# Moving the normalisation's two elementwise passes from VectorE to GpSimd in a post-LayerNorm transformer layer

## The chip, the cores and the metric

The kernel runs on all 8 cores of one Trainium2 chip, each core on its own 2048 of the 16384 token rows, with no traffic between the cores. The time is device microseconds of the slowest core. The hardware profiler also took one execution, whose trace of the slowest core (core 3) is what is read here. An instruction is named by its line in the kernel: L1282 is the instruction issued at line 1282. Engines: PE is TensorE, DVE is VectorE, ACT is ScalarE, POOL is GpSimd, and SP is SyncE, which only issues transfers here.

## What is computed

One layer: attention, residual, LayerNorm, a gated feed-forward with ternary weights, residual, LayerNorm.

```python
def _layernorm(x, axis=-1, eps=1e-5):
    m = jnp.mean(x, axis=axis, keepdims=True)
    v = jnp.var(x, axis=axis, keepdims=True)
    return (x - m) / jnp.sqrt(v + eps)

...
x = _layernorm(x + _L0_attn_ref(x, Wq, Wk, Wv, Wo), axis=-1)
x = _layernorm(x + _L0_ffn_ref(x, w1, w2, w3), axis=-1)
```

Here x is 2 x 8192 x 2048 in float32. `_L0_attn_ref` projects to q, k and v, rotates a part of q and k, and applies softmax attention and the output projection. `_L0_ffn_ref` rounds its weights to -1, 0 and 1 and computes (sigmoid(x w1) * x w2) w3. There are 16 heads, and the feed-forward is 5632 wide.

## The kernel before

Activations lie transposed: 128 partitions hold 128 of the 2048 features, and tokens run along the free axis. So a LayerNorm sums over partitions. It does so with matmuls against a vector of ones, which leave the sum and the sum of squares as one row of 512 tokens; five small DVE instructions and two ACT instructions turn these into -mean and 1/std, two matmuls spread each over 128 partitions into PSUM, and two ACT copies bring them to SBUF as `nm_sb` and `rs_sb`. Then every feature block j (16 of them) is normalised with two passes, `y = y + nm_sb` and `out = y * rs_sb`, each on 128 x 512 elements in float32. These two passes, for one block a "pair" below, are what the change is about.

Everything is written as one instruction stream for each engine, in program order, with semaphores between the engines. No scheduler reorders anything: an instruction that waits holds up all that stands behind it on its engine, transfers too. On DVE, ACT and POOL every instruction also waits for the one before it on the same engine, by a chain semaphore (Vch, Sch, Gch).

- **P0 and P1** (projections, weight statistics, attention) are not touched.
- **P3** (`emit_p3`) is the output projection and the first LayerNorm. It goes over 4 chunks t of 512 tokens. In each it runs 16 units, one for each block j: POOL issues the load of the weights `wot` (L916), SP that of the residual `xto` (L921), PE runs 16 matmuls (L933), DVE adds the residual (L945) and casts (L953), ACT squares (L955), and PE adds to the two sums (L964, L967). The weights have two buffers, so the load for unit u waits until unit u-2 has left PE; the PSUM tiles also have two buffers, so PE runs at most two units ahead of L945. After 16 units come the statistics (L974 to L1005) and the 16 pairs (L1015, L1017). SP stores each result to `x1scr` (L1019), from two staging buffers. In POOL's stream and in SP's, the loads of chunk t+1 stand behind all that chunk t issued there.
- **P4** (`emit_p4`) is the feed-forward and the second LayerNorm, in two halves of 1024 tokens. Each half loads `x1scr` (SP, L1074), and runs 44 steps in which POOL loads `w1t` and `w2t` (L1085, L1089), ACT and DVE quantise them (L1100 to L1113), and PE multiplies (L1128, L1133). Then it multiplies with `w3` (L1177), adds the residual (L1191) and writes the sum to `y2scr` in HBM. At the end of a half come, for each of two token chunks tc, the statistics (L1237 to L1268) and 16 pairs (L1282, L1285). Here the data come back from HBM: SP issues load j (L1278), the pair runs, SP issues store j (L1288), and only behind it in SP's stream stands load j+1.

```python
                    aw = [("p4fs", f4), ("p4ev", self.val("p4ev"))] + spill_done
                    if len(fin_rec) >= 2:
                        aw.append(fin_rec[-2])
...
                            waits=aw, inc=f"p4y2r{par}", inc_amt=16)
```

So the first load of a chunk waits for the statistics too (`f4` is the second ACT copy, L1268).

Of the kernel before, what the change touches and what calls it, by code (L numbers as in the profile page):

```python
# [55 lines left out]
class KB:  # L56
# [829 lines left out]
    def emit_p3(self):  # L886
# [22 lines left out]
        for t in range(4):  # L909
            for j in range(16):  # L910
# [8 lines left out]
                        waits=ww, inc=f"p3dma{par}", inc_amt=16)  # L919
# [3 lines left out]
                        waits=xw, inc=f"p3xd{par}", inc_amt=16)  # L923
# [17 lines left out]
                ybuf = self.f32v(o_y[j], 512)  # L941
                sttw = [("p3mm", mm), xd_]
                if t >= 1:
# [3 lines left out]
                        waits=sttw, inc="p3ev")  # L947
# [23 lines left out]
            while p3pend:  # L971
                p3pend.pop(0)()
            sw = [("p3smm", self.val("p3smm"))]
            self.op("vector", lambda E: E.tensor_scalar(  # L974
# [27 lines left out]
            st3 = self.val("p3st")  # L1002
            self.op("scalar", lambda E: E.copy(out=self.nm_sb, in_=self.pv(1024, 512)),
                    waits=[("p3st", st3)])
            self.op("scalar", lambda E: E.copy(out=self.rs_sb, in_=self.pv(1536, 512)),  # L1005
                    inc="p3st")
            st4 = self.val("p3st")
            for j in range(16):
# [4 lines left out]
                if len(x1st_rec) >= 2:  # L1013
                    aw.append(x1st_rec[-2])
                self.op("vector", lambda E, y=ybuf: E.tensor_tensor(  # L1015
                    out=y, in0=y, in1=self.nm_sb, op=ALU.add), waits=aw)
                self.op("vector", lambda E, y=ybuf, o=x1s: E.tensor_tensor(  # L1017
                    out=o, in0=y, in1=self.rs_sb, op=ALU.mult), inc="p3a")
# [12 lines left out]
    def emit_p4(self):  # L1031
# [38 lines left out]
        for half in range(2):  # L1070
# [163 lines left out]
            for tc in range(2):  # L1234
                sbase = 3072 if tc == 0 else 2048
                sw = [("p4smm", self.val("p4smm"))]
                self.op("vector", lambda E, sb=sbase: E.tensor_scalar(  # L1237
# [28 lines left out]
                self.op("scalar", lambda E: E.copy(out=self.nm_sb, in_=self.pv(1024, 512)),  # L1266
                        waits=[("p4fs", f3)])
                self.op("scalar", lambda E: E.copy(out=self.rs_sb, in_=self.pv(1536, 512)),  # L1268
                        inc="p4fs")
                f4 = self.val("p4fs")  # L1270
                for j in range(16):
# [4 lines left out]
                    if len(fin_rec) >= 2:  # L1276
# [4 lines left out]
                            waits=aw, inc=f"p4y2r{par}", inc_amt=16)  # L1281
                    self.op("vector", lambda E, y=y2: E.tensor_tensor(  # L1282
                        out=y, in0=y, in1=self.nm_sb, op=ALU.add),
                            waits=[(f"p4y2r{par}", self.val(f"p4y2r{par}"))])
                    self.op("vector", lambda E, y=y2, o=outst: E.tensor_tensor(  # L1285
                        out=o, in0=y, in1=self.rs_sb, op=ALU.mult), inc="p4a")
# [71 lines left out]
```

How the kernel before makes its waits and increments, by code:

```python
        def fn(E, SH, _w=tuple(phys_waits), _mk=make, _u=upd):  # L90
            for s, v in _w:
                E.wait_ge(SH[s], v)
            ins = _mk(E)
            if _u is not None:
                ins.then_inc(SH[_u[0]], _u[1])
# [52 lines left out]
        def fn(E, SH, _w=tuple(fw)):  # L148
            for s, v in _w:
                E.wait_ge(SH[s], v)
```

## Time and profile before

| | us |
|---|---|
| median of 2 runs | 12654.13 (12580.48 and 12727.78) |
| the profiled execution | 12302.35 |
| its span, core 3 | 12300.4 |
| spans of the 8 cores | 12165.6 to 12300.4 |
| P0 and P1 | about 7946 |
| P3 | about 592 |
| P4, two halves | about 3762 |

The table's stages are read from the trace of core 3. The span is the time from its first instruction to its last, 2 us less than the time of the same execution. The two timed runs lie 2.3% and 3.5% above the profiled one.

### The profile page before, as it was taken

How to read it: one execution, taken by the hardware profiler on the slowest of the kernel's cores; microseconds unless marked ns; L12 is line 12 of the kernel's file. 1: busy time of each engine (PE TensorE's matmuls, PEld its weight loads, DVE VectorE, ACT ScalarE, POOL GpSimd, SP SyncE). 2: the span in 40 equal slices, each digit the busy share in tenths (PEclk: the TensorE clock that was granted, in tenths of full speed). 3: DMA queues.
4: the chain of work that ended last, by engine and by line, in shares of the span. 5: the costliest groups of instructions: out<-in, count | busy, mean ns of one | idle time of the engine just before them, and what ended most of it. 6: DMA issues, size and time to landing. Idle time of an engine off the chain costs nothing.

```text
span 12300.4 us, 106356 instructions; the slowest of 8 cores (12165.6 to 12300.4 us)
## 1 busy us (share of the span) xinstructions
PE 8438.9 (69%) x34596; PEld 3306.7 (27%) x34596; DVE 4556.7 (37%) x4760; ACT 3940.6 (32%) x3777; POOL 456.6 (4%) x409
## 2 busy tenths in 40 slices
PE   6768668777766088888888888855555681555582
PEld 2223223323322033333333333221222230222231
DVE  2403304214013177777777777633111101111101
ACT  2012012011132266666666666501333200333200
POOL 0000000000000000000000000011000000000000
PEclk9889889888878599999999999977777895777886
DMA  7446355364364400100100100176222223222222
GB/s 140 101 92 142 86 105 120 77 121 104 73 126 97 130 17 27 40 14 27 40 14 27 40 14 27 22 101 106 75 75 75 76 79 87 73 75 75 81 77 61
DMA packets 833313, 904.52 MB, mean 74 GB/s; under 512 B 412672, under 2 KB 713728, under 8 KB 808960
## 3 DMA queue, kind: packets, MB, share of 16 engines
q0 software_dynamic: 471232, 356.54, 17.3%
q1 hardware_dynamic: 361536, 541.18, 14.2%
q8 instruction: 285, 4.67, 0.2%
q14 instruction: 260, 2.13, 0.1%
HBM read 908.07 MB, written 161.48 MB: 87 GB/s over the span
## 4 chain that ended last, share of the span: by engine, by line
PE 50%; ACT 15%; DMA 15%; DVE 10%; issue 4%; another core or an unknown queue 3%; SPq 2%; ACTq 0%; DVEq 0%; POOL 0%; POOLq 0%
PE pp L597 7%; PE pp L430 7%; ACT arena L815 7%; PE pp L800 6%; PE pp L1128 6%; PE pp L805 5%; PE pp L1133 5%; PE pp L1177 5%; DMA arena<-w3t 3%; PE pp L838 2%; DMA arena<-wvt 2%; PE pp L834 2%; DMA arena<-y2scr 2%; DVE arena L317 2%
## 5 line engine op out<-in xcount | busy, mean ns | idle before, releaser
L825 DVE TENSOR_TENSOR arena<-arena 128x1024 f32<-128x1024 f32 x2016 | 2469.4, 1225 | 529.4 <-ACT arena L815 430.5
L815 ACT ACTIVATE arena<-pp,arena 128x1024 bf16<-128x1024 f32 x2048 | 2282.6, 1115 | 886.8 <-PE pp L838 585.9
L430 PE MATMUL pp<-arena 128*128 128x512 bf16 x7680 | 1808.6, 392 | 347.0 <-DMA arena<-wkt 279.9
L800 PE MATMUL pp<-arena 128*128 128x512 bf16 x4096 | 1586.5, 387 | 270.5 <-ACT arena L815 113.2
L1128 PE MATMUL pp<-arena 128*128 128x512 bf16 x2816 | 807.7, 451 | 1230.4 <-DVE arena L1113 1055.1
L805 PE MATMUL pp<-arena 128*128 128x512 bf16 x4096 | 1589.8, 388 | 0.0
L597 PE MATMUL pp<-arena 128*128 128x512 bf16 x4096 | 922.0, 389 | 290.9 <-DMA arena<-wvt 290.9
L430 PEld LDWEIGHTS pp<-arena 128*128 128x128 bf16 x7680 | 739.3, 100 | 1340.5 <-issue 574.6
L317 DVE TENSOR_REDUCE arena<-arena 128x1 f32<-128x2816 f32 (+1 forms) x108 | 298.1, 2760 | 1548.5 <-DMA arena<-w3t 549.4
L834 PE MATMUL pp<-arena 128*128 128x512 bf16 x2048 | 780.6, 381 | 29.8 <-ACT arena L815 29.5
L838 PE MATMUL pp<-arena 128*128 128x512 bf16 x2048 | 778.1, 380 | 0.0
L1128 PEld LDWEIGHTS pp<-arena 128*128 128x128 bf16 x2816 | 309.5, 112 | 1716.4 <-issue 1505.1
L800 PEld LDWEIGHTS pp<-arena 128*128 128x128 bf16 x4096 | 399.5, 98 | 1361.1 <-issue 1126.7
L1177 PE MATMUL pp<-arena 128*128 128x512 bf16 x2816 | 681.0, 405 | 93.3 <-DMA arena<-w3qg 93.1
L1143 DVE TENSOR_TENSOR arena<-pp,arena 128x512 bf16<-128x512 f32 x176 | 121.7, 691 | 1465.0 <-ACT arena L1140 1465.0
L604 ACT CAST arena<-pp 128x512 bf16<-128x512 f32 x256 | 150.0, 586 | 1600.7 <-PE pp L597 1600.7
L1133 PE MATMUL pp<-arena 128*128 128x512 bf16 x2816 | 636.5, 379 | 0.0
L597 PEld LDWEIGHTS pp<-arena 128*128 128x128 bf16 x4096 | 407.5, 100 | 804.8 <-issue 346.0
L1140 ACT ACTIVATE arena<-pp 128x512 f32<-128x512 f32 x176 | 105.1, 597 | 1478.3 <-PE pp L1133 1478.3
L462 DVE TENSOR_REDUCE arena<-pp 1x1 f32<-1x512 f32 x400 | 271.5, 679 | 735.9 <-PE pp L454 610.9
L805 PEld LDWEIGHTS pp<-arena 128*128 128x128 bf16 x4096 | 400.3, 98 | 272.0 <-issue 36.3
L484 ACT CAST arena<-pp 128x512 bf16<-128x512 f32 x256 | 150.0, 586 | 966.2 <-PE pp L430 966.2
(124 smaller groups left out, 5106.7 us busy)
## 6 DMA issues: line engine op xcount, KB each, us to landing
arena<-w3t SPq DMA_DIRECT2D x88, 1024.0 KB, 5.8
arena<-w1t POOLq DMA_DIRECT2D x88, 1024.0 KB, 8.0
arena<-w2t POOLq DMA_DIRECT2D x88, 1024.0 KB, 10.0
arena<-wkt POOLq DMA_DIRECT2D x96, 512.0 KB, 10.0
kscr<-arena SPq DMA_DIRECT2D x384, 128.0 KB, 2.0
arena<-w1t SPq DMA_DIRECT2D x32, 1408.0 KB, 6.6
arena<-w2t SPq DMA_DIRECT2D x32, 1408.0 KB, 6.7
arena<-w3qg SPq DMA_DIRECT2D x32, 1408.0 KB, 13.0
```

The costliest lines, as they stand in the source:

```text
L317: self.op("vector", lambda E, n=ncols: E.tensor_reduce(out=self.gred_tmp, in_=gt[:, 0:n], axis=AX.X, op=ALU.add, apply_absolute_value=True ...
L430: self.op("tensor", lambda E, f=f, ps=ps, t=wk, lo=tok_lo, n=ntok: E.matmul(ps, t[:, f * 128:(f + 1) * 128], xh[:, f * 2048 + lo: f * 2048 ...
L597: self.op("tensor", lambda E, f=f, ps=psV, tb=tb, t=wv: E.matmul(ps, xh[:, f * 2048 + tb * 128: f * 2048 + tb * 128 + 128], t[:, f * 512:( ...
L800: kn=kn, qn=qn: E.matmul(ps[:, hf * 512:(hf + 1) * 512], kn[:, kb * 128:(kb + 1) * 128], qn[:, q0:q0 + 512], start=True, stop=False), waits=w)
L805: kr=kr, qr=qr: E.matmul(ps[:, hf * 512:(hf + 1) * 512], kr[:, kb * 128:(kb + 1) * 128], qr[:, q0:q0 + 512], start=False, stop=True),
L815: self.op("scalar", lambda E, ps=psS, pt=ptile: E.activation(out=pt, in_=ps, func=AF.Exp, bias=self.negmh_bc, scale=1.0), waits=ew, inc="p ...
L825: self.op("vector", lambda E, pt=ptile: E.tensor_tensor(out=lacc, in0=lacc, in1=pt, op=ALU.add), waits=lw, inc="p1l")
L834: self.op("tensor", lambda E, pt=pt, kb=kb, vh=vh2, vo=vo: E.matmul(self.pv(2048, 512), vh[:, kb * 256 + vo:kb * 256 + vo + 128], pt[:, 0: ...
L838: self.op("tensor", lambda E, pt=pt, kb=kb, vh=vh2, vo=vo: E.matmul(self.pv(2560, 512), vh[:, kb * 256 + vo:kb * 256 + vo + 128], pt[:, 51 ...
L1128: self.op("tensor", lambda E, f=f, ps=psA, tc=tc, w1q=w1q: E.matmul(ps, w1q[:, f * 128:(f + 1) * 128], x1h[:, f * 1024 + tc * 512: f * 102 ...
L1133: self.op("tensor", lambda E, f=f, ps=psB, tc=tc, w2q=w2q: E.matmul(ps, w2q[:, f * 128:(f + 1) * 128], x1h[:, f * 1024 + tc * 512: f * 102 ...
L1177: self.op("tensor", lambda E, f=f, ps=psF, tc=tc, jj=jj: E.matmul(ps, w3sl[:, f * 512 + jj * 128: f * 512 + jj * 128 + 128], hsb[:, f * 10 ...
```

## The change

The two passes of both LayerNorms are issued on `gpsimd` in place of `vector`: 64 pairs in P3 and 64 in P4, 256 instructions. Everything that DVE's own order used to guarantee is now a wait: the first statistics instruction (L974, L1237) waits for the earlier statistics to be used up, and the ACT copy that overwrites `nm_sb` (L1003, L1266) waits until the last pairs that read it are done.

```diff
-            sw = [("p3smm", self.val("p3smm"))]
+            sw = [("p3smm", self.val("p3smm")), ("p3st", self.val("p3st"))]
...
             self.op("scalar", lambda E: E.copy(out=self.nm_sb, in_=self.pv(1024, 512)),
-                    waits=[("p3st", st3)])
+                    waits=[("p3st", st3), ("p3a", self.val("p3a")), ("p4a", self.val("p4a"))])
...
-                self.op("vector", lambda E, y=ybuf: E.tensor_tensor(
+                self.op("gpsimd", lambda E, y=ybuf: E.tensor_tensor(
                     out=y, in0=y, in1=self.nm_sb, op=ALU.add), waits=aw)
-                self.op("vector", lambda E, y=ybuf, o=x1s: E.tensor_tensor(
+                self.op("gpsimd", lambda E, y=ybuf, o=x1s: E.tensor_tensor(
                     out=o, in0=y, in1=self.rs_sb, op=ALU.mult), inc="p3a")
...
-                sw = [("p4smm", self.val("p4smm"))]
+                sw = [("p4smm", self.val("p4smm")), ("p4fs", self.val("p4fs"))]
...
                 self.op("scalar", lambda E: E.copy(out=self.nm_sb, in_=self.pv(1024, 512)),
-                        waits=[("p4fs", f3)])
+                        waits=[("p4fs", f3), ("p4a", self.val("p4a"))])
...
-                    self.op("vector", lambda E, y=y2: E.tensor_tensor(
+                    self.op("gpsimd", lambda E, y=y2: E.tensor_tensor(
                         out=y, in0=y, in1=self.nm_sb, op=ALU.add),
                             waits=[(f"p4y2r{par}", self.val(f"p4y2r{par}"))])
-                    self.op("vector", lambda E, y=y2, o=outst: E.tensor_tensor(
+                    self.op("gpsimd", lambda E, y=y2, o=outst: E.tensor_tensor(
                         out=o, in0=y, in1=self.rs_sb, op=ALU.mult), inc="p4a")
```

The first place is POOL's stream in P3. Before, it holds the 64 weight loads in one run, and the first loads of P4 right behind them:

```order
L754 MEMSET arena 128x8192 [waits Gch]
L916 DMA arena<-wot 128x16x128 [waits Vch]
L916 DMA arena<-wot 128x16x128
L916 DMA arena<-wot 128x16x128 [waits p3mm] x62
L1085 DMA arena<-w1t 128x16x128 [waits p3mm]
L1089 DMA arena<-w2t 128x16x128
```

Now the 16 pairs of chunk 0 stand between its loads and those of chunk 1, and so at every chunk's end:

```order
L916 DMA arena<-wot 128x16x128 [waits Vch]
L916 DMA arena<-wot 128x16x128
L916 DMA arena<-wot 128x16x128 [waits p3mm] x14
L1015 TENSOR_TENSOR arena<-arena 128x512 [waits Vch,Sch,p3st,Gch]
L1017 TENSOR_TENSOR arena<-arena 128x512 [waits Gch]
...
L1015 TENSOR_TENSOR arena<-arena 128x512 [waits p3x11,Gch]
L1017 TENSOR_TENSOR arena<-arena 128x512 [waits Gch]
L916 DMA arena<-wot 128x16x128 [waits p3mm] x16
```

The two loads that used to be issued while the pairs ran are moved behind them. In the same way the loads of `w1t` and `w2t` for a half of P4 now stand behind the pairs of P3's last chunk, and behind the 32 pairs of the first half.

The second place is DVE's stream at the end of a half of P4. Before, the pairs of chunk tc=0 stand between the statistics of the two chunks:

```order
L1237 TENSOR_SCALAR arena<-pp 1x512 [waits p4smm,Vch]
...
L1247 TENSOR_SCALAR arena<-arena 1x512 [waits Vch]
L1282 TENSOR_TENSOR arena<-arena 128x512 [waits p4y2r0,Vch]
L1285 TENSOR_TENSOR arena<-arena 128x512 [waits Vch]
...
L1237 TENSOR_SCALAR arena<-pp 1x512 [waits Vch]
```

Now the second chunk's statistics follow the first's, with a wait for ACT and PE (p4fs) in front:

```order
L1237 TENSOR_SCALAR arena<-pp 1x512 [waits p4smm,Vch]
...
L1247 TENSOR_SCALAR arena<-arena 1x512 [waits Vch]
L1237 TENSOR_SCALAR arena<-pp 1x512 [waits Vch,Sch,p4fs]
...
L1247 TENSOR_SCALAR arena<-arena 1x512 [waits Vch]
L1104 TENSOR_TENSOR arena<-arena 128x2048 [waits Sch,p4mm,Vch]
```

So the statistics of tc=1 no longer stand behind 32 passes. PE's stream is the same as before.

## Rows read from the trace of the kernel before

**Rows 1.** The page: the chain that ended last, by engine.
```profile
PE 50%; ACT 15%; DMA 15%; DVE 10%; issue 4%; another core or an unknown queue 3%; SPq 2%; ACTq 0%; DVEq 0%; POOL 0%; POOLq 0%
```
**Rows 2.** Windows: us, busy and count of PE, PEld, DVE, ACT, POOL; PEclk, DMA share, GB/s.
```profile
8062.00:8110.00 48.00, 13.47 (x41) 4.78 (x40) 26.78 (x39) 3.15 (x5) 3.43 (x3) 0.66 0.46 74
10171.00:10423.00 252.00, 8.79 (x13) 2.57 (x12) 54.52 (x78) 14.96 (x14) 3.44 (x3) 0.51 0.38 97
```
**Rows 3.** Groups by line: busy us, mean ns, then idle before and its releasers.
```profile
L1282 DVE TENSOR_TENSOR arena<-arena 128x512 f32<-128x512 f32 x64 | 44.3, 692 | 344.7 <-DMA arena<-y2scr 344.7
L1015 DVE TENSOR_TENSOR arena<-arena 128x512 f32<-128x512 f32 x64 | 44.3, 692 | 62.1 <-DMA x1scr<-arena 30.5 <-ACT arena L1005 29.0 <-DVE arena L1017 2.4
L1285 DVE TENSOR_TENSOR arena<-arena 128x512 f32<-128x512 f32 x64 | 44.3, 692 | 7.0 <-DVE arena L1282 0.5
```
**Rows 4.** Groups by line and form, POOL alone.
```profile
L754 POOL MEMSET arena<- 128x8192 bf16 x1 | 6.9, 6928 | 0.1
L754 POOL MEMSET arena<- 128x2048 bf16 x2 | 3.6, 1809 | 345.8 <-DMA w3qg<-arena 345.7
```
**Rows 5.** Timeline, P4's first pair: start us, length us, instruction, [idle before].
```profile
10189.40 0.69 DVE L1282 TENSOR_TENSOR arena<-arena 128x512 f32<-128x512 f32 x1 [11.66 <-DMA arena<-y2scr]
10190.96 0.34 SPq L1288 DMA_DIRECT2D out<-arena  x1
10191.35 0.42 SPq L1278 DMA_DIRECT2D arena<-y2scr  x1
```
**Rows 6.** Timeline, between the pairs of tc=0 and tc=1, first half.
```profile
10289.19 0.68 DVE L1237 TENSOR_SCALAR arena<-pp 1x512 f32<-1x512 f32 x1
...
10298.42 0.59 ACT L1266 COPY arena<-pp 128x512 f32<-128x512 f32 x1 [4.09 <-PE pp L1262]
...
10299.86 0.32 SPq L1278 DMA_DIRECT2D arena<-y2scr  x1
```
**Rows 7.** Timeline, P3: SP's run of 16 stores in each chunk.
```profile
8077.30 32.62 SPq L1019 DMA_DIRECT2D x1scr<-arena  x16
...
8218.28 32.55 SPq L1019 DMA_DIRECT2D x1scr<-arena  x16
...
8367.11 32.40 SPq L1019 DMA_DIRECT2D x1scr<-arena  x16
...
8511.77 26.38 SPq L1019 DMA_DIRECT2D x1scr<-arena  x16
```
**Rows 8.** The chain in order of time, P3: start us, length us, what.
```profile
8037.64 7.99 DMA arena<-wot
...
8128.35 5.30 PE pp L933 x16
...
8141.49 5.32 PE pp L933 x16
...
8272.71 6.49 PE pp L933 x16
...
8417.98 5.32 PE pp L933 x16
```
**Rows 9.** Timeline, the start of P4's two halves.
```profile
8559.55 6.41 PE L1128 MATMUL pp<-arena 128*128 128x512 bf16 x16 [50.94 <-DMA arena<-x1scr]
...
10405.50 0.43 SPq L1074 DMA_DIRECT2D arena<-x1scr  x1
...
10422.69 4.99 PE L1128 MATMUL pp<-arena 128*128 128x512 bf16 x16 [124.36 <-DMA arena<-x1scr]
```
**Rows 10.** The page: issues, KB each, median us from issue to landing.
```profile
arena<-w1t POOLq DMA_DIRECT2D x88, 1024.0 KB, 8.0
arena<-w2t POOLq DMA_DIRECT2D x88, 1024.0 KB, 10.0
```
**Rows 11.** Groups by line: a sign pass and a quantising add of P4.
```profile
L1108 ACT ACTIVATE arena<-arena 128x2048 bf16<-128x2048 f32 x88 | 176.1, 2001 | 267.5 <-DVE arena L1104 267.5
L1104 DVE TENSOR_TENSOR arena<-arena 128x2048 bf16<-128x2048 bf16 x88 | 107.8, 1225 | 307.7 <-ACT arena L1102 307.5
```

## The prediction

> **What bounds the kernel now.** I read the page first. The chain that ended last is half PE, then ACT and DMA, with DVE at 10% and POOL at 0% [rows 1]. An average over stages says little about 256 instructions, so I went to the stretches where they run, by windows. In a chunk's end in P3 (48 us) PE is busy 13.5 us and POOL 3.4; between the halves of P4 (252 us) PE is busy 8.8 us and POOL 3.4 [rows 2]. There nothing else works: the pairs are on the path, and no matmul hides them. It is also where POOL looks free, so the question is what the pairs cost there, and what they push back.
>
> What ends the waits differs between the two places [rows 3]. In P4 each of 64 pairs waits for its own load from `y2scr` (344.7 us in all, 5.4 each), and the timeline shows a closed ring: L1282 starts at 10189.40, the store is issued 1.56 us later, and the next load only behind it at 10191.35 [rows 5]. Load, two passes, store issue, next load: a pass that gets longer makes the ring longer by just that. In P3 the data are in SBUF and the pairs wait little (30.5 us for staging buffers, 29.0 for the statistics): the passes themselves are most of it.
>
> **The cost of a pass on POOL.** On DVE one takes 0.692 us [rows 3]. No row shows a two-input pass on POOL, so I bound it. POOL's memsets take 1.809 us for 2048 bf16 elements and 6.928 for 8192 [rows 4]: 0.833 ns for each further element and 0.10 us fixed. One stream of 512 elements would be 0.53 us; that is the lower end, 0.16 under DVE. Three streams (two read, one written) that take turns, each float32 element counted as two bf16 ones, would be 0.10 + 3 x 512 x 2 x 0.833 ns = 2.66 us; that is the upper end. If an element costs the same in either type, reads in turn with the write beside them give 0.10 + 0.85 = 0.95 us, and all three in turn 1.38 us. The memsets are the only rows of this engine, and I see no reason for counting bytes rather than elements, so I take the middle of these two, 1.15 us. Call x what a pair gains in length: 2 x (1.15 - 0.69) = 0.92 us, between -0.33 and +3.94. The chain semaphore costs a gap on POOL as it does on DVE; I take it as equal.
>
> Twice the DVE row would be 1.38 us, which is my three streams in turn. The Trainium skill speaks against the change: its GPSIMD Engine Reference, in Performance versus the Vector engine, says that a two-input elementwise operation is about half as fast on GPSIMD, since its two reads share one port, and gives 4497 ns against 2293 ns for 2048 float32 elements. A quarter of 4497 ns is an estimate of 1.12 us, by which the sum below would be 7 us less; its ratio of 1.96 on our row is an estimate of 1.36 us, by which it would be the first rival. No row here shows which.
>
> **The terms.**
>
> 1. *P4's pairs.* 64 rings, each longer by x: 64 x 0.92 = 59 us. All are on the path: the 32 of the first half too, since `x1scr` for the second half is loaded by SP behind them (10405.50), and PE waits 124 us for it [rows 9].
>
> 2. *P3's pairs.* SP's 16 stores of a chunk are issued over 32.6, 32.6, 32.4 and 26.4 us [rows 7], 15 steps each. The last chunk's pace, 1.76 us, is that of the passes with little waiting. The three before it run at 2.17, since transfers of `wot` then share the DMA engines with the stores. On POOL no `wot` is under way then (next term), so all four would run at 1.76 + x = 2.68, which also gives each store longer to land: 40.2 us. That is +7.7 for three and +13.8 for the last, and x more in each for the first pair: 3 x 8.6 + 14.7 = 41 us. In general this term is 64x - 18.
>
> 3. *Loads behind the pairs in P3.* Before, the loads for units 0 and 1 of the next chunk are issued as the last units end, those for 2 and 3 while the pairs run, so units 2 and 3 start at once when the residual has come. Unit 4, the first that waits for its weights, starts 18.4, 21.9 and 18.5 us after the last store is issued (8128.35 - 8109.92, 8272.71 - 8250.83, 8417.98 - 8399.51) [rows 7, 8]. After the change the load for unit 0 is issued only when the pairs are done. It lands 8.0 us later, and from there two units take 13.1 us, bound by such loads (8141.49 - 8128.35) [rows 8]: unit 4 starts at 7.8 + 26.3 = 34.1 us. The loss is 15.7 + 12.2 + 15.6 = 43 us. What DVE gains does not help: L945 is free to run, but there is no product for it. The bounds are 30 us, if loads land in 6 us when nothing else moves, and 48.
>
> 4. *Statistics of tc=1 in P4.* From L1237 at 10289.19, right after the last pair of tc=0, to the load at 10299.86 are 10.7 us, of which the two ACT copies and the issue at the end are 1.4 (from 10298.42) [rows 6]. With DVE free, all up to the copies is done while POOL works through tc=0's pairs. Only the copies, which wait for these pairs, stay: -9.2 us for each half, -18.4 us. The gain is bounded by these 9.2, and nothing queued behind the waiting copy on ACT is needed earlier: the sign passes of the next half have no weights yet. In P3 no such gain exists, since a chunk's statistics need its own matmuls.
>
> 5. *Loads of `w1t` and `w2t` behind the pairs.* Before, they had long landed, and PE waited for `x1scr`: 21.4 us after the last store of P3 was issued, and 17.2 us after the issue of the load in the second half [rows 7, 9]. Now they are issued when the last pair ends and land 8.0 and 10.0 us after issue [rows 10]; then four sign passes and two adds follow, 4 x 2.0 + 2 x 1.2 = 10.5 us with little between [rows 11]: about 20 to 21 us, if `x1scr`, 4 MB, does not slow them. It will: 6 MB share the engines where 4 MB took 17.2 us, which at the same rate is 26 us. I take +8 for the first half and +11 for the second, 19 us; the bounds are 0 and 30, the upper end with the weights landing only behind `x1scr`.
>
> The new waits in front of L974 and L1237 are met when they are reached in P3 (the last broadcast is a whole chunk old), and in P4 lie inside term 4. Other edits have no price.
>
> Sum: 59 + 41 + 43 - 18 + 19 = 144; as a formula it is 128x + 26. Against the profiled execution's own 12302 us that is 12446. The median of the runs shown is 12654, 352 us higher, for which the trace has no row; I put the same 144 us on top of it: 12798 us, or 1.1%.
>
> **Rivals.**
>
> - *A pass takes 1.38 us*, twice the DVE row. Then x = 1.38 and the sum is 128 x 1.38 + 26 = 203 us: 12857, 1.6%. For it: two reads and a write in turn. The skill's ratio of about two, in the same place of the GPSIMD Engine Reference, would put it here. Chance 0.20.
> - *POOL is much slower*, over 1.6 us a pass: this is the case on the other side. With x above 1.78 the sum passes 253 us, which is 2%. Two float32 reads in turn counted by bytes are 0.10 + 1.71 = 1.81 us, x = 2.24, +313 us: 12967. For it: the memset's rate is known for a 2-byte type alone. Against it: it needs POOL at 2.6 times DVE's time. Chance 0.14.
> - *The freed DVE pays.* If the next chunk's units could run beside the pairs, the idle 33 us of PE in each of three boundaries would go: terms 2 and 3 become about 15 - 99 = -84, and the sum 59 - 84 - 18 + 19 = -24 us: 12630. For it: PE is idle there [rows 2]. Against it: both streams that feed these units, POOL's and SP's, hold their loads behind the pairs. Chance 0.04.
> - *POOL is as fast as DVE* or faster: x near 0 gives +26, x = -0.33 gives -16: 12638 to 12680. Chance 0.07.
>
> **How the numbers follow.** The forecast keeps 0.55, with x from 0.5 to 1.2 and so +90 to +180. The range reaches down through the two cheap cases to 12600, which is -54, about their lower end with terms 3 and 5 at theirs, and up to the 1.81 us pass, 12965; about 0.12 lies outside. A measurement of this kernel can tell some 2% (253 us) from no change. Faster by more than that: 0.01, since even the lowest bound is under 1%. Slower: 0.14 for the slow pass and 0.01 for terms 3 and 5 at their worst beside a dear pass, 0.15. Within 2%: 0.84.
>
> **What would show each step.** In the trace after: the mean of L1015 and L1282 on POOL (1.15; the price of a pass); the run of 16 stores, 40 us in every chunk (term 2); POOL's first `wot` issue behind the last L1017, and unit 4 34 us after the last store (term 3); L1237 of tc=1 starting while the pairs of tc=0 run, and 1.4 us between the last pair and the load (term 4); PE's first L1128 waiting for L1113 or for `x1scr`, 25 to 30 us after the last pair (term 5). The forecast is wrong if the pass is off by half a microsecond, or if a ring in P4 grows by something other than the two passes, such as a slower hand-over from POOL to SP.

## The result, and the profile after

| | before | changed |
|---|---|---|
| median of all its runs, us | 12677.99 (10 runs, 12275.55 to 12846.53) | 12550.24 (11 runs, 12444.93 to 12963.89) |
| comparable runs, changed / before | | **1.0153**, 95% interval 1.0105 to 1.0201 |
| span of the profiled execution's slowest core | 12300.4 | 12444.2 |
| span of its median core | 12194.7 | 12421.6 |

Some executions of either kernel run at a lower clock and take some per cent longer, so only undisturbed ones are compared, and the two medians of all runs say nothing. On 12302 us the ratio is +188 us (+129 to +247): slower, and by less than the 2% that was called a difference, which the upper end of the interval (2.01%) just reaches. The two profiled spans differ by 144 us, the very sum of the prediction, but that is chance: core 3 of the kernel before ended 106 us behind its median core, core 4 of the changed one 23 us behind. Between median cores it is +227 us. I work below with medians over the eight cores of the times between named instructions:

| stretch, us | before | changed | difference |
|---|---|---|---|
| P3 (first L933 to P4's first L1128) | 603.0 | 724.8 | +121.8 |
| closing block of the first half (first `y2scr` load to the issue of the last store) | 185.3 | 228.4 | +43.1 |
| last store's issue to the second half's first L1128 | 18.9 | 29.4 | +10.5 |
| closing block of the second half (to the end) | 185.7 | 233.5 | +47.8 |

These four make 223 of the 227 us. The page of the changed kernel (span; busy times; the chain by engine):

```profile
span 12444.2 us, 105745 instructions; the slowest of 8 cores (12388.3 to 12444.2 us)
PE 8328.7 (67%) x33908; PEld 3296.5 (26%) x34596; DVE 4378.3 (35%) x4504; ACT 3938.0 (32%) x3777; POOL 779.3 (6%) x665
PE 50%; ACT 15%; DMA 14%; DVE 8%; issue 5%; another core or an unknown queue 3%; POOL 3%; SPq 2%; ACTq 0%; DVEq 0%; POOLq 0%
```

Against [rows 1], POOL has come onto the chain with 3% and DVE has left it with 2: the pairs stayed on the path when they changed engine. One window between the halves (us; busy time and count of PE, PEld, DVE, ACT, POOL; granted clock, DMA share, GB/s), core 4:

```profile
10290.00:10545.00 255.00, 3.75 (x4) 1.16 (x4) 0.00 (x0) 1.35 (x3) 80.42 (x64) 0.50 0.35 82
```

It answers to the second of [rows 2]: DVE does nothing at all now, PE next to nothing (3.75 us), and POOL is busy for under a third of the time. The groups by line (busy us, mean ns of one, idle before and its releasers), core 4:

```profile
L1282 POOL TENSOR_TENSOR arena<-arena 128x512 f32<-128x512 f32 x64 | 80.8, 1262 | 1196.5 <-DMA arena<-y2scr 1196.5
L1285 POOL TENSOR_TENSOR arena<-arena 128x512 f32<-128x512 f32 x64 | 80.7, 1260 | 9.2
L1017 POOL TENSOR_TENSOR arena<-arena 128x512 bf16<-128x512 f32 x64 | 80.6, 1260 | 9.2
L1015 POOL TENSOR_TENSOR arena<-arena 128x512 f32<-128x512 f32 x64 | 80.6, 1260 | 115.5 <-ACT arena L1005 106.9
L1266 ACT COPY arena<-pp 128x512 f32<-128x512 f32 x4 | 2.3, 585 | 228.5 <-POOL arena L1285 220.1 <-PE pp L1262 8.4
```

A pass takes 1260 ns, whether it writes float32 or bf16; on DVE it took 692 [rows 3]. The idle time of 1196.5 us in front of L1282 is no cost to read: POOL waits there through each half as well, where before DVE had other work. The timeline of core 4 (start us, length us, instruction, [idle before]) shows the places of [rows 5 to 9]:

```profile
8050.22 42.42 SPq L1019 DMA_DIRECT2D x1scr<-arena  x16
8092.19 2.36 POOL L916 DMA_DIRECT2D arena<-wot  x2
8101.84 9.93 PE L933 MATMUL pp<-arena 128*128 128x512 bf16 x32 [55.97 <-DMA arena<-wot]
...
8131.00 5.30 PE L933 MATMUL pp<-arena 128*128 128x512 bf16 x16 [3.82 <-DMA arena<-wot]
...
8590.00 42.42 SPq L1019 DMA_DIRECT2D x1scr<-arena  x16
8631.97 1.21 POOL L1085 DMA_DIRECT2D arena<-w1t  x1
8634.13 0.37 SPq L1074 DMA_DIRECT2D arena<-x1scr  x1
8644.95 2.00 ACT L1100 ACTIVATE arena<-arena 128x2048 bf16<-128x2048 f32 x1 [58.02 <-DMA arena<-w2t]
8656.33 5.71 PE L1128 MATMUL pp<-arena 128*128 128x512 bf16 x16 [70.80 <-DVE arena L1113]
...
10294.08 1.26 POOL L1282 TENSOR_TENSOR arena<-arena 128x512 f32<-128x512 f32 x1 [4.37 <-DMA arena<-y2scr]
10295.48 1.26 POOL L1285 TENSOR_TENSOR arena<-arena 128x512 f32<-128x512 f32 x1
10296.81 0.34 SPq L1288 DMA_DIRECT2D out<-arena  x1
10297.24 0.39 SPq L1278 DMA_DIRECT2D arena<-y2scr  x1
...
10398.81 1.26 POOL L1285 TENSOR_TENSOR arena<-arena 128x512 f32<-128x512 f32 x1
10400.16 0.58 ACT L1266 COPY arena<-pp 128x512 f32<-128x512 f32 x1 [109.98 <-POOL arena L1285]
10401.60 0.32 SPq L1278 DMA_DIRECT2D arena<-y2scr  x1
...
10558.21 5.39 PE L1128 MATMUL pp<-arena 128*128 128x512 bf16 x16 [264.04 <-DVE arena L1113]
```

The reader is to see four things. The ring is the same, with 3.16 us from the first pass to the next load where it had 1.95 [rows 5]. PE waits 56 us at a P3 boundary for `wot`, whose loads POOL issues only at 8092.19, behind the last pass; unit 4 starts 38.4 us after the last store (8131.00 - 8092.64). Between tc=0 and tc=1 only the copies are left, 1.5 us from the store's issue to the load. And both halves of P4 now wait for quantised weights (L1113), not for `x1scr` as in [rows 9].

### The profile page after: what moved, and what is told of

Read it like the earlier page. It is cut to its first block, busy times and chain, and to the rows that moved or that the text cites. A ratio compares the mean times of both kernels' runs of the same rounds, so it can differ in the third digit from the quotient of the medians.

```text
span 12444.2 us, 105745 instructions; the slowest of 8 cores (12388.3 to 12444.2 us)
## 1 busy us (share of the span) xinstructions
PE 8328.7 (67%) x33908; PEld 3296.5 (26%) x34596; DVE 4378.3 (35%) x4504; ACT 3938.0 (32%) x3777; POOL 779.3 (6%) x665
## 4 chain that ended last, share of the span: by engine, by line
PE 50%; ACT 15%; DMA 14%; DVE 8%; issue 5%; another core or an unknown queue 3%; POOL 3%; SPq 2%; ACTq 0%; DVEq 0%; POOLq 0%
PE pp L430 7%; PE pp L597 7%; ACT arena L815 7%; PE pp L1128 6%; PE pp L800 6%; PE pp L805 5%; PE pp L1133 5%; PE pp L1177 5%; DMA arena<-w3t 3%; PE pp L838 2%; DMA arena<-y2scr 2%; DMA arena<-wot 2%; DMA arena<-wvt 2%; PE pp L834 2%
## 5 line engine op out<-in xcount | busy, mean ns | idle before, releaser
L1128 PE MATMUL pp<-arena 128*128 128x512 bf16 x2762 | 799.9, 452 | 1404.0 <-DVE arena L1113 1398.9
L805 PE MATMUL pp<-arena 128*128 128x512 bf16 x4096 | 1589.1, 388 | 50.9 <-DMA arena<-kscr 25.8
L1128 PEld LDWEIGHTS pp<-arena 128*128 128x128 bf16 x2816 | 310.8, 113 | 1881.1 <-issue 1667.8
L834 PE MATMUL pp<-arena 128*128 128x512 bf16 x1970 | 750.3, 381 | 29.7 <-ACT arena L815 29.4
L604 ACT CAST arena<-pp 128x512 bf16<-128x512 f32 x256 | 149.8, 585 | 1590.1 <-PE pp L597 1590.1
L1143 DVE TENSOR_TENSOR arena<-pp,arena 128x512 bf16<-128x512 f32 x176 | 121.8, 692 | 1439.6 <-ACT arena L1140 1439.6
L933 PE MATMUL pp<-arena 128*128 128x512 bf16 x1001 | 289.4, 452 | 312.5 <-DMA arena<-wot 310.2
```

Of the source, the lines that this page charges most:

```text
L805: kr=kr, qr=qr: E.matmul(ps[:, hf * 512:(hf + 1) * 512], kr[:, kb * 128:(kb + 1) * 128], qr[:, q0:q0 + 512], start=False, stop=True),
L834: self.op("tensor", lambda E, pt=pt, kb=kb, vh=vh2, vo=vo: E.matmul(self.pv(2048, 512), vh[:, kb * 256 + vo:kb * 256 + vo + 128], pt[:, 0: ...
L1128: self.op("tensor", lambda E, f=f, ps=psA, tc=tc, w1q=w1q: E.matmul(ps, w1q[:, f * 128:(f + 1) * 128], x1h[:, f * 1024 + tc * 512: f * 102 ...
```

## The experiments

Each leaves the computation as it is. "Land" is the time from a `y2scr` load's issue to the first pass, "pass part" from there to the next load's issue; both are medians over cores of each core's mean. A diff is against the changed kernel where nothing else is said.

### One place at a time

In `x1_p4_only` P3's pairs are back on DVE, in `x2_p3_only` P4's are. The lines are those of P3; in P4 the same two words change:

```diff
-                self.op("gpsimd", lambda E, y=ybuf: E.tensor_tensor(
+                self.op("vector", lambda E, y=ybuf: E.tensor_tensor(
...
-                self.op("gpsimd", lambda E, y=ybuf, o=x1s: E.tensor_tensor(
+                self.op("vector", lambda E, y=ybuf, o=x1s: E.tensor_tensor(
```

> Only the pairs of P4 on POOL, those of P3 back on DVE. Stage figures are medians over the 8 cores, from before and after: the closing block of a half of P4 (first y2scr load to last store issued) took 185 us before and 228 (first half) after, a ring 5.46 and 7.14 us. Theory (a ring pays the length of its two passes, 2 x (1.26 - 0.69) and two gaps, 1.24 us, and nothing else): each block is longer by 32 x 1.24 - 9.2 = 30 us, the start of the second half by 10; P3 stays at 603 us; in all +70 us. Rival (on POOL the ring also pays a slower hand-over or slower loads, as the 1.68 us between the two traces suggest): blocks +43 to +48, in all +100 us.

> Only the pairs of P3 on POOL. Theory (the terms of the two LayerNorms are independent): P3, from its first L933 to the first L1128, takes 725 us as after the change against 603 before, so +120 us; the closing blocks of P4 stay at 185 us, with 10.7 us between the pairs of the two chunks. Rival (P3's loss comes from the whole change, by transfers or clock): P3 well under 725. The two kernels, P4 alone and P3 alone, should add up to the change: about +190 to +230.

On their chip the kernel before took 12245 us (median of four comparable runs). `x1_p4_only`: 12307, +62. Its blocks took 215.6 and 218.8 us (+30 and +33), the second half started after 29.4 us, as in the changed kernel, and P3's runs of stores were those of before (the whole of P3, 636 us at a granted clock of 0.74 over that trace, is not comparable with the 603). `x2_p3_only`: 12309 and 12393, +64 and +148; its P3 took 707.0 us (+104, where I had expected +120), its runs of stores 42.1 us in all four chunks, and the second half started after 18.8. Its closing blocks did not stay at 185 us: they took 203.9 and 199.0, with the pairs on DVE, because its `y2scr` loads landed late (3.84 us where the kernel before has 3.45, in the table below). The two halves add up to +126 to +210 us, beside the change's +188. So each half of the change brings its own loss, and the late weights of the second half belong to P4's pairs. The groups of `x1_p4_only` (core 6) show the two engines in one kernel:

```profile
L1282 POOL TENSOR_TENSOR arena<-arena 128x512 f32<-128x512 f32 x64 | 81.2, 1269 | 1220.6 <-DMA arena<-y2scr 1220.6
L1015 DVE TENSOR_TENSOR arena<-arena 128x512 f32<-128x512 f32 x64 | 44.3, 692 | 63.2 <-DMA x1scr<-arena 31.2 <-ACT arena L1005 29.0 <-DVE arena L1017 2.9
```

### The loads, and the statistics

`x3_loads_first` issues the next loads ahead of the pairs (P4's first `w1t` and `w2t` likewise):

```diff
+            if t < 3:
+                wot_load(16 * t + 16)
+                wot_load(16 * t + 17)
+            else:
+                self.p4_first_load()
             for j in range(16):
```

> The changed kernel, but POOL issues the next stage's first loads (wot for units 0 and 1 of the next chunk, w1t and w2t of the next half) ahead of the pairs. Theory (the loads queued behind the pairs cost 53 us in P3 and 10 + 2 us at the starts of the halves): unit 4's end after the last store of a chunk goes from 44 back to 26 us, P3 from 725 to about 672, the start of the second half from 29.4 to 19 us, in all -65 us against the changed kernel, and what is left, about +125 against before, is the price of the passes. Rival (POOL's descriptor work for the loads is itself slowed beside the passes, or the stores suffer): P3 stays above 690.

P3 fell from 724.8 to 685.7 us, and the start of the second half from 29.4 to 21.0; P4's first start is that of before again (21.9). The one comparable run took 12400. Its timeline on core 1:

```profile
8032.10 1.14 POOL L912 DMA_DIRECT2D arena<-wot  x1 [8.21 <-PE pp L940]
8036.18 1.15 POOL L912 DMA_DIRECT2D arena<-wot  x1 [2.94 <-PE pp L940]
...
8047.69 8.63 PE L940 MATMUL pp<-arena 128*128 128x512 bf16 x32
8049.38 1.26 POOL L1027 TENSOR_TENSOR arena<-arena 128x512 f32<-128x512 f32 x1 [12.04 <-ACT arena L1012]
...
8094.10 2.35 POOL L912 DMA_DIRECT2D arena<-wot  x2
```

The products of units 0 and 1 (8047.69) now run before the pairs begin. Units 2 and 3 still get their weights at 8094.10, behind the pairs, since all loads stand in POOL's order. The order of issue on POOL, not POOL's work as such, cost 39 us of P3 and 8 of P4; 83 us of P3's loss stay with the loads in front. I had expected 53 us back in P3. At the three boundaries unit 4's residual add (L945) ends 29 us after the last store, against 43 to 44 in the changed kernel and 25 to 26 before, which is 43 of the 53 us; what is left fits the late weights of units 2 and 3. Elsewhere P3 was some 6 us slower than in the changed kernel, 2 of them in the last run of stores (43.9 us).

`x4_stats_first` is the kernel before, on DVE, with tc=0's pairs emitted behind the statistics of tc=1:

```diff
+                if tc == 1:
+                    pairs0()
                 self.op("scalar", lambda E: E.copy(out=self.nm_sb, in_=self.pv(1024, 512)),
```

> All pairs on DVE as before, but in P4 the statistics of the second token chunk stand ahead of the pairs of the first, on DVE, ACT and PE; only the copies into nm_sb and rs_sb wait for those pairs. Theory (the 9.2 us that the change wins in each half is a matter of order, not of the engine): the gap goes from 10.7 to 1.5 us in each half, in all -18 us. Rival: the five statistics instructions ahead of the first pair delay it and give 3.5 us of each 9.2 back, -11 us; or the gain needs a free DVE, 0.

The gap between the pairs fell from 10.7 to 1.6 us, and the blocks from 185.3 and 185.7 to 175.0 and 173.7. It had no comparable run, so it is read by blocks alone. The one gain of the change is a matter of order: DVE gives it too, without POOL.

### What a pass costs in the ring

`x5_third_pass` issues the second pass of P4's pairs twice, on POOL:

```diff
+                    self.op("gpsimd", lambda E, y=y2, o=outst: E.tensor_tensor(
+                        out=o, in0=y, in1=self.rs_sb, op=ALU.mult))
                     self.op("gpsimd", lambda E, y=y2, o=outst: E.tensor_tensor(
                         out=o, in0=y, in1=self.rs_sb, op=ALU.mult), inc="p4a")
```

> The changed kernel with the second pass of every P4 pair done twice on POOL (the same product again, so the output is the same). The runs so far give a ring of 6.4 to 6.6 us on cores whose loads are not disturbed with the passes on POOL, and 5.3 with them on DVE. Theory (the ring pays the passes one for one): one pass and its gap more, 1.40 us, ring 7.8 to 8.0, each closing block +45 us (32 x 1.40), +90 in all. Rival (part of the pass hides beside the load, or the excess of the first comparison is a cost of each POOL instruction): ring +0.7 or less, or +1.7 and more.

```profile
10340.00 1.26 POOL L1282 TENSOR_TENSOR arena<-arena 128x512 f32<-128x512 f32 x1 [3.85 <-DMA arena<-y2scr]
10341.41 1.26 POOL L1285 TENSOR_TENSOR arena<-arena 128x512 f32<-128x512 f32 x1
10342.81 1.26 POOL L1287 TENSOR_TENSOR arena<-arena 128x512 f32<-128x512 f32 x1
10344.14 0.34 SPq L1290 DMA_DIRECT2D out<-arena  x1
10344.57 0.38 SPq L1278 DMA_DIRECT2D arena<-y2scr  x1
```

This is its timeline on core 5: 4.57 us from the first pass to the next load, 1.41 more than with two. The blocks took 258 us, which is only 30 and 25 more than in the changed kernel's first trace, where I had expected 45: the loads landed 0.47 us earlier in this one, and 32 x (1.41 - 0.47) is 30. Taken apart, the ring reads:

| us | pass part | land |
|---|---|---|
| before; `x4_stats_first`; `x2_p3_only` (DVE) | 2.00; 2.01; 2.01 | 3.45; 3.39; 3.84 |
| changed; `x1_p4_only`; `x3_loads_first`; `x12_changed_again` (POOL) | 3.18; 3.18; 3.19; 3.18 | 3.93; 3.54; 3.34; 3.56 |
| `x5_third_pass` (POOL, three passes) | 4.59 | 3.46 |

The pass part is the same on all eight cores to 0.02 us. POOL adds 1.18 us to a ring: 2 x 0.568 for the passes and 0.04 for the gaps. "Land" is 3.2 to 5.0 us, by core and by run, and goes with neither engine: so the 0.48 us by which the changed kernel's first trace is worse is hardly the change's. Here a theory of mine fell, that a ring on POOL has a slower hand-over to SP.

### The ring opened

`x6_ring_open_dve` and `x7_ring_open_pool` keep two loads under way: load j+2 is issued after store j, and the wait for the staging buffer moves to the second pass. Pairs of P4 on DVE in the first, on POOL in the second; P3's pairs are on DVE in `x6` and on POOL in `x7`.

```diff
+                y2_load(0)
+                y2_load(1)
                 for j in range(16):
...
+                            waits=[fin_rec[-2]] if len(fin_rec) >= 2 else [], inc="p4a")
...
+                    if j + 2 < 16:
+                        y2_load(j + 2)
```

> All pairs on DVE. In P4 SP issues the loads of pairs 0 and 1 first and then load j+2 right behind store j, so that one load is under way while a pair runs; the first pass waits for the load, the second for the staging buffer. Theory (the ring, load to pass to store to load, is what P4's closing blocks are): the ring falls from 5.3 us to half of load plus pair plus issue, (3.5 + 1.6 + 0.4) / 2 = 2.75 us, a block from 185 to about 105 us, in all -160 us. Rival (the loads are bound by the memory, not by being asked for late): they land later as two are under way, ring above 4, -70 us or less.

> The changed kernel, pairs on POOL, with the same order of loads. Theory: the ring is (3.5 + 2.8 + 0.4) / 2 = 3.35 us, a block falls from 228 to about 115 us, in all -220 us against the changed kernel; the engine's price falls to 0.6 us for a pair, half of what it is in the closed ring, and with it the distance between POOL and DVE in P4 from 77 to about 40 us. Rival (POOL's two passes, 2.8 us with gaps, bound it alone): 2.8 us, 100 us for a block.

A step took 3.27 us on DVE and 3.78 on POOL, where the closed rings took 5.46 and 7.14; the blocks took 121.3 and 120.8 us on DVE, 127.8 and 131.7 on POOL. Comparable runs: 12116 and 12241, the kernel before 12227 and 12281. So, with what POOL's order gains on the statistics counted in, POOL costs 30 us a block and more in a closed ring, 7 to 11 in an open one. With the same order of the statistics on both engines it is 41 and 45 us closed (`x1_p4_only` against `x4_stats_first`) and 6 and 7 open (`x7` against `x8` below). Most of the price of the slower engine was the price of having no second load. I had expected 2.75 us and 105 us on DVE, 3.35 and 115 on POOL. The loads are why: this is the DMA view of `x6_ring_open_dve`, core 2, in the second block (KB each, median us from issue to landing):

```profile
arena<-y2scr SPq DMA_DIRECT2D x32, 256.0 KB, 4.5
```

The same core and stretch of the kernel before have 3.2 us. Two loads under way each take longer: by the mean of all `y2scr` loads, median of cores, 4.4 us against 3.3. `x8_dve_open_stats` puts `x4`'s order and `x6`'s ring together:

```diff
+                if tc == 1:
+                    pairs0()
...
+                    y2_load(0)
+                    y2_load(1)
```

> All pairs on DVE, P4 with the open order of loads (ring 3.3 us when tried alone, block 121 us) and the statistics of the second chunk ahead of the first chunk's pairs (-9.2 us for each half when tried alone); the loads no longer wait for the statistics. Theory (the two gains add, and the first load of each chunk leaves the path, 3 us each): a closing block of 121 - 9 - 6 = 106 us, in all about -160 us against before. Rival (with loads early, statistics late again bound it): 115 us, -140.

The gap went to 0.4 us, yet the blocks took 121.7 and 125.0 us, no less than in `x6`. Part of that is where a block begins: its first load is now issued 5 and 11 us earlier, ahead of the statistics, and the first pass waits for these all the same (18.7 us after the second half's last `w3` product, 18.2 in `x6`). From that product to the end it is 129.4 us, against 135.6 in `x6`, and from the first half's last `w3` product to the second half's first L1128 151.6 against 156.1. So 4.5 and 6 us came of the 10 that the gap gave, and nothing of the 3 for the earlier load; the steps took 3.35 us in place of 3.27, 2.4 us over 30 of them. That the rate of the loads is the bound is my reading of it; no run here separates that from the stores' share.

### Both engines in P3

`x9_split_p3` has the loads in front and gives 6 of 16 pairs of P3 to POOL, 10 to DVE; the wait for the staging buffer moves to the second pass, as in `x6`; P4's pairs are on DVE.

```diff
+                eng = "gpsimd" if j % 8 in (2, 5, 7) else "vector"
+                self.op(eng, lambda E, y=ybuf: E.tensor_tensor(
```

> P4's pairs on DVE. In P3, 10 of the 16 pairs of a chunk run on DVE and 6 (j = 2, 5, 7, 10, 13, 15) on POOL, with the next loads of wot, w1t and w2t ahead of them. The 16 stores of a chunk were issued over 32 us on DVE alone and 42 us on POOL alone. Theory A (the engines work side by side): the larger of 10 x 1.65 and 6 x 2.8, 17 us, or about 20 with the two staging buffers. Theory B (a two-input pass on DVE and one on POOL exclude each other, as the Trainium skill says in SBUF - State Buffer, Who interferes with whom): 10 x 1.65 + 6 x 2.8 = 33 us, and single DVE passes in the trace as long as a POOL pass.

The runs of stores took 25.8, 25.9, 26.5 and 26.1 us: neither of the two theories' numbers. It had no comparable run; P3 took 606 us (603 before), and 597 to 606 on the four cores whose granted clock in that stage was that of before (0.77 to 0.78). Its groups on core 0, and six lines of its timeline on core 3 (L1027 and L1029 are the two passes):

```profile
L1027 DVE TENSOR_TENSOR arena<-arena 128x512 f32<-128x512 f32 x40 | 39.9, 997 | 32.8 <-ACT arena L1012 29.1
L1027 POOL TENSOR_TENSOR arena<-arena 128x512 f32<-128x512 f32 x24 | 38.1, 1587 | 50.6 <-ACT arena L1012 47.7
L1029 DVE TENSOR_TENSOR arena<-arena 128x512 bf16<-128x512 f32 x40 | 37.1, 926 | 23.0 <-DMA x1scr<-arena 20.9
L1029 POOL TENSOR_TENSOR arena<-arena 128x512 bf16<-128x512 f32 x24 | 33.7, 1402 | 40.0 <-DMA x1scr<-arena 40.0
```

```profile
8493.01 1.71 POOL L1027 TENSOR_TENSOR arena<-arena 128x512 f32<-128x512 f32 x1 [12.01 <-ACT arena L1012]
8493.71 1.57 DVE L1029 TENSOR_TENSOR arena<-arena 128x512 bf16<-128x512 f32 x1
8495.38 0.69 DVE L1027 TENSOR_TENSOR arena<-arena 128x512 f32<-128x512 f32 x1
...
8504.33 0.69 DVE L1029 TENSOR_TENSOR arena<-arena 128x512 bf16<-128x512 f32 x1 [1.19 <-DMA x1scr<-arena]
8504.40 1.74 POOL L1027 TENSOR_TENSOR arena<-arena 128x512 f32<-128x512 f32 x1
8505.12 1.56 DVE L1027 TENSOR_TENSOR arena<-arena 128x512 f32<-128x512 f32 x1
```

A DVE pass that starts while POOL is in one takes 1.57 us, the next, alone, 0.69. Both engines are slower together: DVE 997 and 926 ns on average against 692, POOL 1587 and 1402 against 1260.

The passes take turns, as theory B has it, and the one that starts first is not slowed. Over all cores, 390 DVE passes began while POOL was in none: each took 0.69 us, the 204 in which a POOL pass began too. Of the 250 that began within a POOL pass, 240 ended 0.55 us after it. A POOL pass that began within a DVE pass (302 of them) took 1.26 us and what the DVE pass had still to run, less 0.14 us, to within 0.01. So the one that comes second waits until the first is done but for its last 0.14 us. Theory B's 33 us were too many because they added up whole pairs with their gaps: the passes alone are 20 x 0.692 + 12 x 1.26 = 29 us, part of which runs before the first store is issued.

A chunk's pairs took no less than on DVE alone where no `wot` is moved beside them (26.4 us in before's last chunk [rows 7]); that the other three fell from 32.5 to 26 goes with the loads put in front and the wait moved as well, and this run does not separate the three. The Trainium skill names such a conflict: SBUF — State Buffer, in Who interferes with whom, says that a DVE instruction with two SBUF inputs contends with a GpSimd one that reads SBUF, and calls the contention an exclusive lock. This trace agrees, with the 0.55 and 0.14 us above.

### The pairs woven into the next stage

If the loss is that nothing works beside the pairs, the remedy is no engine but a place. `x10_woven` leaves all pairs on DVE and puts each chunk's pairs one by one into the units of the next chunk, and the first half's 32 pairs into the weight steps of the second half; the last block has the open ring.

```diff
             for j in range(16):
+                if t >= 1:
+                    late_pair(j)
...
+                if half == 1 and o < 32:
+                    late_pair4(o)
```

> All pairs on DVE, but off the path: in P3 pair j of chunk t runs just ahead of unit j's L945 in chunk t+1; in P4 the 32 pairs of the first half run one for each of the first 32 weight steps of the second half (nm_sb and rs_sb of the second chunk have buffers of their own), and the last half has the open order of loads. Theory (what counts is that PE has nothing to do while pairs run): P3's three waits of 32 us for pairs go, 603 to about 510 us; the first half's closing block falls from 185 to about 30 us of statistics; the last one to 106: in all -330 us against before, 2.7%. Rival (the woven pairs delay the quantising adds L1104 and L1113, on which PE waits in P4, and L945 in P3): 48 us for 32 pairs in the second half, which would take 1675 us in place of 1627, and about 50 in P3: -230 us.

Four comparable runs took 11885 to 11903 us; the kernel before took 12386 in its one comparable run on that chip and 12206 at best on any. Its page, and windows of core 3 (P3; first half; second half):

```profile
span 11888.3 us, 106311 instructions; the slowest of 8 cores (11813.9 to 11888.3 us)
PE 53%; ACT 15%; DMA 13%; DVE 9%; issue 4%; another core or an unknown queue 3%; SPq 2%; ACTq 0%; DVEq 0%; POOL 0%; POOLq 0%
```

```profile
7959.00:8483.00 524.00, 327.59 (x1170) 117.96 (x1169) 201.58 (x278) 58.39 (x84) 75.36 (x66) 0.82 0.88 126
8483.00:10126.00 1643.00, 1041.38 (x4295) 433.77 (x4293) 209.94 (x249) 430.16 (x305) 98.52 (x86) 0.82 0.26 77
10126.00:11769.00 1643.00, 1042.59 (x4296) 434.45 (x4296) 255.75 (x316) 427.00 (x304) 98.54 (x86) 0.82 0.29 85
```

The median core's span is 11862.2 us, 333 less than before's, as expected (330). P3 takes 518 us (603), with the DMA engines busy for 88% of it, which is likely its bound now; no run tests that. The first closing block is gone: from the first half's last `w3` product to the second half's first product are 37.5 us, where it was 220.5. The second half has 46 us more DVE work than the first in windows of one length, and the pairs' loads and stores in it, and still takes 1610.6 us from its first product to its last `w3` product (median of cores). Before it took 1612.3, so the pairs are hidden altogether. From that last product to the end are 134.0 us, where it was 200.6: this part is the open ring's.

`x11_woven_pool` moves the first half's woven pairs to POOL.

```diff
+                eng = "gpsimd" if half == 0 else "vector"
```

> The kernel before it (woven), with the first half's 32 pairs of P4 on POOL, all others on DVE. Theory (off the path the slower engine costs nothing): the second half's weight steps and w3 product take 1627 us as before, and the time is that of the woven kernel within 15 us. Rival (a POOL pass holds up DVE's adds with two SBUF inputs, or the weight loads that stand behind the pairs on POOL): +1 to +1.4 us for each of 32 steps, +30 to +45 us in that stretch.

11899 us in its comparable run. On cores 4 to 7, whose granted clock in its trace (0.86) is that of `x10_woven`, the second half took 1609 to 1616 us by the same two products, as on DVE. Off the path the slower engine cost nothing, and freeing DVE brought nothing.

### The changed kernel once more

> The changed kernel once more, on the chip of the woven kernels. Stage figures of the first trace: P3 725 us against 603, closing blocks 228 and 234 against 185, start of the second half 29 against 19, ring 7.1 against 5.5. Theory (the passes are longer by 1.24 us a pair, and what is over that in the ring is disturbance of the loads, as on two of the eight cores before the change): ring 6.4 to 6.6 on most cores, blocks near 212, in all +180 us against before. Rival (the excess belongs to POOL): ring 7.1 again, +220 us.

`x12_changed_again` is the changed kernel itself (no edit), beside the kernel before on the chip of `x8` and `x10`: 12548 us against 12386 in the one comparable run each, +1.3%, inside the interval. P3's runs of stores (42.1 us), the start of the second half (29.4) and the gap (1.5) are those of the first trace; the blocks took 213.5 and 222.5, with loads that landed after 3.56 us.

## Why the prediction was nearly right

It forecast +144 us, +1.2% of the profiled execution, within 2%; measured is +1.5%, which on the prediction's base of 12654 us is 12848, inside the range and 50 us above the 12798 forecast. The likeliest case (x from 0.5 to 1.2) is the one that came, at its edge: x is 1.18. By its own formula, 128x + 26, that x gives 177 us; the measured +188 lies just above the +90 to +180 that went with the case.

| term | forecast | measured |
|---|---|---|
| 1, P4's pairs | +59 | +76 (64 x 1.18) |
| 2, P3's pairs | +41 | +51 (stores 46, first pairs 5) |
| 3, loads behind the pairs in P3 | +43 | +53 |
| 4, statistics of tc=1 hidden | -18 | -18 |
| 5, `w1t` and `w2t` behind the pairs | +19 | +13 |
| sum | +144 | +175 |

**The price of a pass was mis-sized**, the step where I took the middle of 0.95 and 1.38 us: 1.15 was 1.26. It is also where the gap after a pass was taken as equal: it is 0.14 us on POOL and 0.11 on DVE. That is 17 us in term 1 and as good as all of term 2's error: 2.80 us a pair where I had 2.68. The Trainium skill's GPSIMD Engine Reference, in Performance versus the Vector engine, would have given an estimate of 1.12 us by its time and 1.36 by its ratio of 1.96; the measured 1.26 us lies between the two, and the ratio here is 1.82.

**Term 2's reading held.** I said that all four runs would take one pace, since no `wot` is moved beside the stores: they took 42.1 us each, where before three took 32 and one 26.

**Term 3 had the mechanism right and the landing too short.** On core 4 the first load took 9.7 us from issue to PE's start (8092.19 to 8101.84), where I took 8.0 as from the chain before; the next four units then took 29.2 us (to 8131.00), where I took 26.3. The load is issued 0.45 us before the last store's issue ends, so unit 4 started 38.4 us after it, not 34.1. Over the three boundaries, by unit 4's residual add, the loss is 17.6, 17.7 and 17.5 us. `x3_loads_first`, which gave 43 of these 53 us back at the boundaries, shows that the order was the cause.

**Term 4 was right to a tenth of a microsecond**: the gap went from 10.7 to 1.5 us. `x4_stats_first` adds that POOL was not needed for it.

**Term 5 was too large**: +2.1 in the first half, where I had 8, and +10.5 in the second, where I had 11. That PE would wait for the quantising is right (8656.33 and 10558.21, `<-DVE arena L1113`). In the first half `x1scr` is itself loaded late on SP (8634.13), so both loads come out nearly together.

**The new waits cost nothing**, as priced: the copy L1266 waits 220 us for POOL, and nothing on ACT was needed meanwhile.

**The rivals.** The 1.38 us pass, a pass over 1.6 us, and POOL as fast as DVE are all refuted by 1260 ns. The freed DVE does not pay in any stretch: its window between the halves is empty. `x10_woven` shows that work beside the pairs was there to be had, but only by another order of issue: of the 333 us by which its median core is ahead, 85 are P3's and 183 the first closing block's, beside 227 that the change lost.

**What is left.** The stretches come to +223, the terms to 175. Of the other 48, about 31 are the late `y2scr` loads of that one trace (64 x 0.48), which `x12_changed_again` and `x1_p4_only` all but lack (0.1 us a load) and `x2_p3_only` has without POOL (0.39); that brings it to 192, beside the 188 of the ratio. About 16 lie in P3's units: a chunk's seventh to sixteenth `wot` loads are issued over 61 to 62 us in the changed kernel, `x3`, `x5` and `x7`, and 57 to 60 before, but 59 in `x2_p3_only`, which has P3's pairs on POOL as well. What makes this is open.

## What to carry to other kernels

An idle engine was worth nothing here for work that stands on the path: look at what runs beside the moved work, and if nothing does, move the work in time and not in place. A closed ring of load, pass, store and next load takes each microsecond of a slower engine one for one; a second load under way was worth more here (64 us a block) than the faster engine (30 and more). Where an engine also issues loads, list what is queued behind the moved work, and expect a gain that comes with a move (here the statistics) to be had from the order alone.

## What the runs showed of the hardware

- A two-input pass of 128x512 takes 1260 ns on POOL and 692 on DVE, for a float32 and for a bf16 output alike. The gap to the next instruction of its chain is 0.14 and 0.11 us.
- Two-input passes from SBUF on both engines take turns (`x9_split_p3`, 640 DVE and 384 POOL passes). The one that starts first is not slowed; the second waits for it, less 0.14 us. On average a DVE pass took 997 and 926 ns, a POOL pass 1587 and 1402.
- With one 256 KB load from `y2scr` under way on a core, the first pass that needs it starts 3.2 to 5.0 us after its issue, by core and run. From issue to landing it is 3.2 us with one and 4.5 with two on core 2 (medians of the second block), 3.3 and 4.4 by the median of cores.
